# A hybrid block's norms from VectorE's statistics instructions, and its routing from the eight-largest and position instructions

## What is computed

```python
def _layernorm(x, axis=-1, eps=1e-05):
    m = jnp.mean(x, axis=axis, keepdims=True)
    v = jnp.var(x, axis=axis, keepdims=True)
    return (x - m) / jnp.sqrt(v + eps)
...
# mixture: 16 experts of width 64 and a shared one, the two best are taken
router_logits = jax.nn.sigmoid(x @ gate_w + gate_b)
expert_values, expert_indices = jax.lax.top_k(router_logits, k=TOP_K)
expert_values = expert_values / jnp.sum(expert_values, axis=-1, keepdims=True)
...
return x + _mlp(x, shared_wg, shared_wu, shared_wd) + expert_weighted
...
# state space: projection, convolution of 3 taps, silu, then
_, y = jax.lax.scan(step, state0, xs)
mu = jnp.mean(y, axis=-1, keepdims=True)
var = jnp.var(y, axis=-1, keepdims=True)
y = (y - mu) * jax.lax.rsqrt(var + 1e-05)
y = y @ W_si + b_si
y = y + D * x_main
y = y * jax.nn.sigmoid(gate)
return y @ W_out + b_out
...
x = L0_attn_a_x
x = x + _L0_attn_a_ref(_layernorm(x, axis=-1), ...)
x = x + _L0_ffn_ref(_layernorm(x, axis=-1), ...)
x = x + _L0_attn_b_ref(_layernorm(x, axis=-1), ...)
x = x + _L0_ffn_ref(_layernorm(x, axis=-1), ...)
```

## Time and profile before

| | |
|---|---|
| median of 3 runs | 878.74 us |
| the profiled execution | 878.15 us |
| its span, first to last instruction | 876.3 us |
| TensorE busy | 779.5 us (89%) |
| VectorE busy | 478.3 us (55%) |
| ScalarE busy | 432.4 us (49%) |
| GpSimd busy | 433.7 us (49%) |
| mean granted clock of TensorE | 0.957 of full speed (2.4 GHz) |

### The profile page before, as it was taken

One profiled execution on the slowest core, in us unless ns is written; L12 is line 12 of the kernel. 1 busy time (PEld: TensorE's weight loads), 2 busy tenths in 40 slices (PEclk: granted clock), 3 DMA queues, 4 the chain that ended last, 5 costly groups with the idle time before them and its releaser, 6 DMA issues. The chain is left out here.

```text
span 876.3 us, 14873 instructions
## 1 busy us (share of the span) xinstructions
PE 779.5 (89%) x6024; PEld 523.5 (60%) x6024; DVE 478.3 (55%) x718; ACT 432.4 (49%) x564; POOL 433.7 (49%) x310
## 2 busy tenths in 40 slices
PE   1689999999999999999999998989899676579998
PEld 1455555555555556565555555968788432558887
DVE  6653554454554455455545511766575685666552
ACT  3344445555544544554554451566565560276543
POOL 2044755674575566558556675143344262133443
PEclk9889999999999999999999999999999785789999
DMA  2000000000000000000000002300000000000000
GB/s 60 7 1 1 7 2 1 7 1 1 8 1 1 7 1 1 8 1 1 1 2 25 1 1 76 87 1 1 1 1 1 0 1 0 1 0 13 7 8 25
DMA packets 18963, 8.14 MB, mean 9 GB/s; under 512 B 7952, under 2 KB 18768, under 8 KB 18896
## 3 DMA queue, kind: packets, MB, share of 16 engines
q1 hardware_dynamic: 18896, 7.20, 3.2%
HBM read 6.15 MB, written 1.05 MB: 8 GB/s over the span
## 5 line engine op out<-in xcount | busy, mean ns | idle before, releaser
L476 DVE TENSOR_REDUCE at_half_max<-at_ring 128x2 f32<-128x1024 f32 (+1 forms) x192 | 177.2, 955 | 120.8 <-PE at_ring L571 104.7
L359 POOL TENSOR_TENSOR all_x<-all_x,at_probs 128x1024 f32<-128x1024 f32 (+3 forms) x128 | 220.4, 1722 | 40.5 <-ACT at_probs L432 25.7
L432 ACT ACTIVATE at_probs<-at_ring 128x1024 f32<-128x1024 f32 x144 | 147.1, 1023 | 145.8 <-PE at_ring L605 127.3
L359 POOL TENSOR_TENSOR all_x<-at_probs 128x768 f32<-128x768 f32 (+1 forms) x32 | 66.9, 2092 | 165.1 <-ACT at_probs L432 164.9
L1128 POOL TENSOR_TENSOR m_prod<-m_gate,m_wb_copy 128x512 f32<-128x512 f32 x64 | 82.4, 1292 | 124.5 <-ACT m_gate L956 124.5
L623 PE MATMUL at_out<-at_probs,at_k_nat 128*64 128x512 f32 (+3 forms) x768 | 140.3, 494 | 1.1 <-DVE a_attn_t L497 0.9
L596 PE MATMUL at_ring<-at_qh,at_kh 64*128 64x512 f32 (+3 forms) x384 | 77.7, 401 | 21.2 <-DVE at_m_rows L488 21.0
L623 PEld LDWEIGHTS at_out<-at_probs,at_k_nat 128*64 128x64 f32 x768 | 49.2, 136 | 66.1 <-issue 59.3
L853 PEld LDWEIGHTS m_acc<-rest_wd,m_hid 128*128 128x128 f32 x576 | 76.6, 195 | 6.2
L956 ACT ACTIVATE m_gate<-m_g 128x512 f32<-128x512 f32 x72 | 43.1, 598 | 73.1 <-PE m_g L845 72.4
L564 PE MATMUL at_ring<-at_kh,at_qh 64*128 64x512 f32 (+3 forms) x384 | 74.8, 395 | 4.0 <-DVE at_half_max L476 2.4
(11 more groups left out here) (224 smaller groups left out, 1408.9 us busy)
## 6 DMA issues: line engine op xcount, KB each, us to landing
all_x<-in_L_attn_a_x SPq DMA_DIRECT2D x8, 256.0 KB, 4.0
at_w_raw<-in_L_attn_a_W_qk SPq DMA_DIRECT2D x8, 128.0 KB, 2.5
out<-all_x SPq DMA_DIRECT2D x4, 256.0 KB, 2.3
a_room<-in_L_attn_a_W_out SPq DMA_DIRECT2D x1, 512.0 KB, 4.0
m_raw_wg<-in_L_ffn_experts_wg SPq DMA_DIRECT2D x1, 512.0 KB, 4.7
m_raw_wu<-in_L_ffn_experts_wu SPq DMA_DIRECT2D x1, 512.0 KB, 4.3
rest_wd<-in_L_ffn_experts_wd SPq DMA_DIRECT2D x1, 512.0 KB, 4.2
rest_w_in<-in_L_attn_b_W_in SPq DMA_DIRECT2D x1, 256.0 KB, 4.3
```

The lines of the kernel that those rows point to most:

```text
L359: return pool.tensor_tensor(sums[:, :, a * P:b * P], left, right, ALU.add)
L432: act.activation(probs[:, :, slot * BANK:(slot + 1) * BANK], pair("S", unit, slot)[:, :, :], ACT.Exp, scale=BETA).then_inc(exp_done, 1)
L476: last = dve.reduce_max(half_max[:, :, i, int(a > 0)], pair("M", unit, m)[:, :, at:at + (b - a) * P], AX.X)
```

## The change

Every norm takes its mean and variance from VectorE's statistics instructions: one `bn_stats` a tile (6 numbers a row) and one `bn_aggr` (mean and variance), and then one `tensor_scalar` a tile, (x - mean) * rstd, with both scalars read from tiles. ScalarE's square goes, and the root adds eps as a bias. In the first layernorm VectorE does each group's statistics and, one group later, its norm. In the mixtures `centre`, `square` and `variance` become `statistics`; `root` is due one step earlier, and so are the steps that follow in `FINISH` by one or two. The routing finds the eight largest of 16 scores (`max`) and their positions (`max_index`) tile by tile, and builds the weights from the first two. In the state space the norm reads PSUM itself, in 8 rows of 64.

```diff
+def row_statistics(dve, stats, moments, x, small, count, done):
+
+    for t in range(x.shape[1]):
+        last = dve.bn_stats(stats[:, t, :], x[:, t, :])
+    last.then_inc(small, 1)
+    dve.wait_ge(small, count + 1)
+    for t in range(x.shape[1]):
+        last = dve.bn_aggr(moments[:, t, :], stats[:, t, :])
+    last.then_inc(done, 1)
+    return count + 1
+
+
+def scale_rows(dve, out, x, moments, rstd, done):
+    for t in range(x.shape[1]):
+        last = dve.tensor_scalar(out[:, t, :], x[:, t, :], moments[:, t, 0:1], rstd[:, t:t + 1], ALU.subtract, ALU.mult)
+    last.then_inc(done, 1)
...
+            def statistics(n):
+                dve.wait_ge(x_loaded[n], 16)
+                count[0] = row_statistics(dve, grp(stats, n), grp(moments, n), grp(k.x, n), small, count[0], varied)
+
+            def norm(n):
+                dve.wait_ge(rooted, n + 1)
+                dve.reciprocal(cols(rstd, n), cols(sd, n)).then_inc(small, 1)
+                count[0] += 1
+                dve.wait_ge(small, count[0])
+                scale_rows(dve, grp(xn, n), grp(k.x, n), grp(moments, n), cols(rstd, n), normed)
...
+            statistics(0)
+            for n in range(1, GROUPS):
+                statistics(n)
+                norm(n - 1)
+            norm(GROUPS - 1)
...
-PREPARE = dict(centre=-21, square=-19, variance=-18, root=-16, norm=-16, residual=-15, turn=-14, high=-13,
+PREPARE = dict(statistics=-21, root=-17, norm=-16, residual=-15, turn=-14, high=-13,
                low=-13, logits=-10, sigmoid=-9, natural=-8, route1=-8, route2=-7, route3=-6, turn_w=-3,
                w_high=-2, w_low=-3)
 
-FINISH = dict(add_up=0, centre=2, square=4, variance=5, root=6, norm=6, turn=7, high=8, low=8)
+FINISH = dict(add_up=0, statistics=2, root=4, norm=4, turn=6, high=7, low=7)
...
-                if piece == "square" and n == 1:
+                if piece == "root" and n == 1:
                     at = PREPARE["sigmoid"]
...
+    def norm(self, dve, n, x):
         dve.wait_ge(self.rooted, n + 1)
         dve.reciprocal(self.rstd[:, :], self.sd[:, :]).then_inc(self.small, 1)
-        dve.wait_ge(self.small, 4 * n + 4)
+        dve.wait_ge(self.small, 2 * n + 2)
         wait(dve, self.turned, n)
-        dve.tensor_tensor(self.xn[:, :, :], self.xc[:, :, :], bcast(self.rstd[:, :], D), ALU.mult)\
-           .then_inc(self.normed, 1)
+        scale_rows(dve, self.xn, x, self.moments, self.rstd, self.normed)
...
-        act.activation(self.sd[:, :], self.var[:, :], ACT.Sqrt).then_inc(self.rooted, 1)
+        act.activation(self.sd[:, :], self.moments[:, :, 1], ACT.Sqrt, bias=eps[:, :]).then_inc(self.rooted, 1)
...
-                        norm.variance(dve, n)
-                        if ahead_of and n == 1 and norm is after:
-                            ahead_of.split_low(dve)
+                        norm.statistics(dve, n, grp(k.x, n))
...
-                        largest(sc, v1, i1, one1)
...
+                        for t in range(PER):
+                            last = dve.max(top[:, t, :], sc[:, t, :])
+                        then(last)
+                        dve.tensor_tensor(den[:, :], top[:, :, 0], top[:, :, 1], ALU.add)
+                        for t in range(PER):
+                            last = dve.max_index(at_top[:, t, :], top[:, t, :], sc[:, t, :])
+                        then(last)
                     elif piece == "route2":
-                        largest(sc2, v2, i2, one2)
+                        dve.tensor_copy(at_f[:, :, :], at_top[:, :, 0:2].rearrange("p t r -> p r t"))
+                        then(dve.reciprocal(rec[:, :], den[:, :]))
+                        dve.tensor_tensor(share[:, :, :], top[:, :, 0:2].rearrange("p t r -> p r t"),
+                                          rec[:, :].unsqueeze(1).to_broadcast([P, 2, PER]), ALU.mult)
+                        then(dve.tensor_tensor(picked[:, :, :, :], f.iota[:, :, :].unsqueeze(1).to_broadcast([P, 2, PER, EXPERTS]),
+                                               at_f[:, :, :].unsqueeze(3).to_broadcast([P, 2, PER, EXPERTS]), ALU.is_equal))
                     elif piece == "route3":
...
+                        then(dve.tensor_tensor(parts[:, :, :, :], picked[:, :, :, :],
+                                               share[:, :, :].unsqueeze(3).to_broadcast([P, 2, PER, EXPERTS]), ALU.mult))
                         wait(dve, wt_ready, n)
-                        dve.tensor_tensor(w[:, :, :], w1[:, :, :], w2[:, :, :], ALU.add).then_inc(w_ready, 1)
+                        dve.tensor_tensor(w[:, :, :], parts[:, 0, :, :], parts[:, 1, :, :], ALU.add).then_inc(w_ready, 1)
...
+                def statistics(h):
 
                     dve.wait_ge(nat_ready, h + 1)
-                    then(dve.tensor_copy(y_nat[:, h, :, :], ps[6 + h][:, :].rearrange("p (t s) -> p t s", s=STATE)))
...
+                    count[0] = row_statistics(dve, stats[:, h, :, :], moments[:, h, :, :], natural(h), link, count[0], varied)
 
                 def norm(h):
                     dve.wait_ge(rooted, h + 1)
                     then(dve.reciprocal(rstd[:, h, :], sd[:, h, :]))
-                    dve.tensor_tensor(y_c[:, h, :, :], y_c[:, h, :, :], bcast(rstd[:, h, :], STATE), ALU.mult)\
-                       .then_inc(normed, 1)
+                    scale_rows(dve, y_c[:, h, :, :], natural(h), moments[:, h, :, :], rstd[:, h, :], normed)
...
+                pool.memset(k.eps[:, :], EPS).then_inc(ident_made, 1)
                 pool.memset(k.ident[:, :], 0.0).then_inc(ident_made, 1)
-                pool.wait_ge(ident_made, 1)
+                pool.wait_ge(ident_made, 2)
```

150 lines of the change are left out of this document (42 added, 108 removed).

## The result

The changed kernel took 868.58 us (median of five runs, 867.95 to 868.9) against 878.74 us for the kernel before in the same comparison: a ratio of 0.988, 95% interval 0.987 to 0.990. It is 10.2 us faster. The forecast was 4.5 us faster, so it named the right sign and less than half of the size; the time lies in the range given, near rival A (869). The profiled execution of the changed kernel has a span of 867.1 us, against 876.3.

A forecast was written before the change was run, and what follows sets the result against it. TensorE, busy 89% of the span, was taken as the bound, so shorter VectorE work pays only where TensorE waits. The terms summed to -4.5 us: 873.65 from the profiled 878.15, 874.2 as median; range 868 to 880, 871 to 877 at 0.5.

The forecast's parts named there:

- rival A: Clean case: routing's GpSimd waits and the stall at 618 go wholly, buffers cover half the table loads; 869 us, chance 0.2.
- Point 1: First layernorm: VectorE does statistics and norm group by group without leaving; 1.5 us faster (-3.2 to +0.5).
- Point 2: First mixture's opening: the norm costs nothing, but the root right behind the sigmoid costs 0.5 us (0 to +1.5).
- Point 3: Mixtures: sigmoid's and root's table loads in consecutive steps delay ScalarE's expert-weight copy; +1.1 us each in second mixture's opening and second group.
- Point 4: First mixture's second group: the stall before m_hid loses 1.4 us, less 1.1 from table loads; -0.8 us (-4.4 to +1.5).
- Point 5: First mixture's last norm, with nothing beside it: 2.95 us instead of 4.73, so -1.8 us (-2.2 to -0.5).
- Point 6: State space: first half's eight scalings out of PSUM cost 1.1 us more, second half gets shorter; 0 in sum (-1.5 to +1.5).
- Point 7: Second mixture's opening, where VectorE is the path: shorter norms and routing start the spreading product 3.1 us earlier (-4.2 to -1.0).
- Point 8: Everything else: other statistics and routes shrink under TensorE for 0; low clock that may follow longer waits, +0.2 us.
- C: Rival, slower: the fixed price of some 125 small instructions on the path exceeds the gain; 885.4 us, chance 0.1.
- B: Rival: the four scalings and GpSimd lock each other out, in the first layernorm and mixture norms; 878.4 us, chance 0.12.
- D: Rival: gains are found, but TensorE's low clock in the openings and the table loads eat them; 878 to 880, chance 0.08.

The follow-up runs named there:

- root_back: The changed kernel with the opening norm's square root due at -16 again, one step later, as before; 863.97 us, ratio 0.9827.
- late_route: The changed kernel with twelve small VectorE copies delaying the first group's routing in both mixtures; 871.86 us, ratio 0.9933.
- root_early: The kernel before with the opening norm's square root moved from -16 to -17, its place in the changed kernel; 884.61 us, ratio 1.0064.
- old_route: The changed kernel with the routing of before, the new norms and their step numbers kept; 877.72 us, ratio 0.9987.
- new_route: The kernel before with the new routing alone, the old norms kept; 872.25 us, ratio 0.9923.
- pair_scale: The changed kernel with one whole-row subtraction and one multiplication for the four scalings, in the first layernorm and both mixtures; 870.47 us, ratio 0.9911.

## Why the prediction was right and wrong

**Point 1, first layernorm** (-1.5): -2.3 by all profiles, -2.4 by the medians. The statistics of a group cost 1.2 us start to start, not 1.6, and a norm 1.3 us alone, up to 2.5 beside GpSimd. Right mechanism, bn_aggr too dear (0.38 for four, priced at 0.56).

**Point 2, first opening** (+0.5): 0. Its low end was right: root_back, with the root in its old place, has the same 34.15 us, and late_route shows nearly 3 us of cover for VectorE there.

**Point 3, table loads behind each other** (+0.5, +1.1, +1.1, less 0.19): right in mechanism, shown by root_back and root_early, and worth 2.8 us by the rows of the two loops and 4.6 by the medians. I had 2.5 in this point and 1.1 more inside point 4. But it is not where I put it: nothing of it lies in the second opening. It lies behind it, where the third step takes 5.46 us (2.73 in root_back) and the first five together 1.1 more than there, and in step 13 of both mixtures, +1.5 each, of which step 14 gives 0.5 back. So two consecutive pairs cost 1.0 to 1.1 in each of three places, and the 1.1 was well priced.

**Point 4, second group of the first mixture** (-0.8): the step that failed first. I let the stall keep 1.6 us and the low clock behind it stay. Both went. VectorE between two `m_hid` is now this:

```profile
610.73 0.87 DVE L85 BATCH_NORM_STATS2 m_after_stats<-all_x 128x6 f32<-128x128 f32 x4
...
612.10 1.12 DVE L96 TENSOR_SCALAR m_before_xn<-all_x,m_before_moments,m_before_rstd 128x128 f32<-128x128 f32 x4
...
613.41 1.25 DVE L1055 TENSOR_TENSOR m_share<-m_top,m_rec 128x8 f32<-128x8 f32 x1
614.58 0.28 DVE L1057 TENSOR_TENSOR m_picked<-rest_iota,m_at_f 128x128 f32<-128x128 f32 x1
614.90 0.69 DVE L1005 TENSOR_TENSOR m_hid<-m_prod,m_u 128x512 f32<-128x512 f32 x1
```

This is 4.2 us from 610.73 to 614.90, not 5.9: the share waited for GpSimd once, 1.1 us, `picked` did not wait. TensorE waited 0.46 us. Stall and low clock were 4.4 us in all by my own reckoning, and step 15 gave nearly that, 7.28 to 3.24, -4.0; I had kept it for rival A. (My -0.8 was -1.4 and +1.1, and 0.5 of the low clock that I did not spell out.) Steps 13, 16, 25 and 34 took back 4.3, less 2.0 in the steps next to them, which were shorter. The last three, the new places of the finishing norm, are in no term: I looked at what the end of the mixture gains from them and not at whose copies they stand in front of.

**Point 5, last norm** (-1.8): -1.9; 2.98 us against 2.95. Right.

**Point 6, state space** (0): the two waits are 6.8 us for 6.9. Right as a sum of a gain and a loss, by two errors that cancel in part: the eight scalings took 2.11 for 1.8, and statistics of eight rows 1.8 for 2.6. The first half's wait grew from 2.04 to 3.47, the second's fell from 4.88 to 3.35.

**Point 7, second opening** (-3.1, with +1.1 of point 3): -4.8. This is the step that failed by most: I took VectorE's shorter chain as the whole of the gain and kept TensorE's own work at its old pace; in the stretch between the two norms it fell from 6.49 us busy to 5.16. 1.1 of 2.8 is point 3's misplaced term. The first norm's end was right, 7.55 us behind the output product instead of 8.83: -1.3 against -1.4. The second norm came 3.1 us earlier, not 1.8: in the stretch ahead of it the granted clock was 1.00 and not 0.81, and route1 was 0.45 shorter than priced. The new norms alone bring 2.8 of the 3.1, at 1.00 too (old_route); how much of that is the shorter chain and how much the clock, no run separates. From there to the spread it was 4.64 us for 6.35, 1.7 less, against 1.3. (My terms for this point, as listed, add to 2.75 and not to 3.1.)

**Point 8, low clock** (+0.2): the wrong sign. I counted the clock as a loss that follows new waits and never as a gain where waits go. Behind its spread at 772 us the kernel before ran at 0.50 until 778.3, 6.8 us of low clock in all; the changed one ran at 1.00 for 7 us and then at 0.50 for 3.4.

**Second mixture's rest** (+1.1): -0.2. The table loads cost 2.0 there (root_back) and the routing gained 2.4 (new_route), which I had put at nothing because it lay under TensorE (point 8); step 6 went from 3.50 to 2.51 us there, and the two waits for `m_hid`, 1.0 us, went.

**Rivals.** A is nearest, and half by luck. Its first reason holds for the stall, though of the routing's waits for GpSimd one of 1.1 us stayed (613.41, and 758.41 in the second opening). Its second, that ScalarE's buffers cover half of the table loads, is contradicted by root_back; the time came to 869 all the same because the second opening and what follows it gained 4.0 us more than the forecast. C is refuted by the prices, MAX8 0.40 and bn_aggr 0.38 for four. B is refuted by pair_scale and by the time. D is in the runs as a part, with no weight in the sum.

**Open.** Whether the interaction of 1.5 to 2 us is the clock and that alone, since no run held it fixed, and what makes the clock fall in the second opening of new_route and pair_scale and not in that of the others. Why root_back gains more in time than in its rows. And what makes the attention differ by 1 us between executions.

## What to carry to other kernels

A part that clears one engine's backlog can be worth more than its own length, and another part can be worth nothing until that is cleared: the new norms brought 1.1 us by themselves and 3.4 on top of the new routing. When steps are renumbered, ask of each which copy or hand-over stands behind it in its engine's queue: here one number, a square root moved one step, took 3 to 5 of some 15 us that were to be had. Whether one operation a tile beats a pair of whole-row operations has to be timed in each place: the pair won where the tiles were small and in PSUM and its first operation found idle time, and lost 1.3 us in the loops of the mixtures, where VectorE had other work waiting. And before a difference between two kernels is put down to the edited instructions, compare the granted clock of the stretch that grew.

## What the runs showed of the hardware

- Four BATCH_NORM_STATS2 of 128 elements take 0.87 us, four BATCH_NORM_AGGREGATE 0.38, four MAX8 of 16 values 0.40, and a value load with its position search starts every 0.15. The aggregates and MAX8 start less than 0.1 apart, like a plain instruction of 4 elements (0.09), though each returns several results.
- Four scalings with two per-row scalars take 1.12 us for 128 elements each out of SBUF and eight take 2.11 for 64 each out of PSUM: about 0.26 start to start either way, so half the elements from PSUM had the price of the whole from SBUF.
- The granted clock fell to 0.50 behind a stretch in which TensorE was busy 2.38 of 7 us, and behind one of 1.24 of 4 us although TensorE had been kept busy shortly before. 3.4 us more at 0.50 made the loop behind the second opening only 0.5 us longer; 5.9 us at 0.71 instead of 4.6 at 1.00 stood in the opening of pair_scale, with nearly the same work (19 and 18 matmuls).
- Twelve products of 512 columns behind 4 us of idle TensorE started every 0.43 us, and every 0.23 behind thirty transposes, with a granted clock of 1.00 in the rows of both.
